# Choosing two of eight experts in two parts, in the stage ahead and behind the first products

## The reference

```python
logits = (xt @ w_gate.T).astype(jnp.float32)
top_logits, top_idx = jax.lax.top_k(logits, TOP_K)          # TOP_K = 2 of 8
top_gates = jax.nn.softmax(top_logits, axis=-1)
gates = (one_hot(top_idx, E) * top_gates[..., None]).sum(axis=1)
for e in range(E):
    h = xt @ w_in[e].T
    y = y + gates[:, e:e + 1] * (h @ w_out[e].T)
# x = x + 0.5 * y
```

## Time and profile before

| | us |
|---|---|
| median of three runs | 1414.59 |
| profiled execution, its own time | 1414.04 |
| its span | 1412.3 |
| PE busy | 1173.9 (83%) |
| DVE busy | 869.1 (62%) |
| ACT busy | 649.0 (46%) |
| POOL busy | 585.5 (41%) |

### The profile page before, as it was taken

The page is one execution under the profiler, slowest core; times in us unless marked ns, Lnnn a source line. Parts: engine busy times, 40 slices in busy tenths (PEclk is TensorE's granted clock), DMA queues, the critical chain, the costliest instruction groups (busy, mean ns, idle before and its releaser), DMA issues. The chain is left out here.

```text
span 1412.3 us, 30262 instructions
## 1 busy us (share of the span) xinstructions
PE 1173.9 (83%) x11551; PEld 686.9 (49%) x11561; DVE 869.1 (62%) x2263; ACT 649.0 (46%) x1346; POOL 585.5 (41%) x727
## 2 busy tenths in 40 slices
PE   3895889886968979999969886846985999898698
PEld 3582444444845645566536534333771233233377
DVE  5146778842155678788535598871177889893205
ACT  1222566651432446766632252421453777685143
POOL 5763244113541669987310112163743033123352
PEclk9997799997968989999989896867995799999699
DMA  7542333105710186666229000013433122110344
GB/s 138 154 113 79 94 105 98 45 11 141 223 41 1 38 231 193 181 190 200 78 39 112 8 2 1 3 46 109 132 95 101 47 80 80 34 37 17 87 143 119
DMA packets 137674, 128.66 MB, mean 91 GB/s; under 512 B 19245, under 2 KB 120377, under 8 KB 137536
## 3 DMA queue, kind: packets, MB, share of 16 engines
q1 hardware_dynamic: 127392, 103.46, 28.0%
q0 software_dynamic: 10080, 23.31, 5.0%
q10 hardware_dynamic: 64, 0.04, 0.0%
HBM read 79.80 MB, written 47.69 MB: 90 GB/s over the span
## 5 line engine op out<-in xcount | busy, mean ns | idle before, releaser
L2803 DVE TENSOR_REDUCE att_maxima<-psum 128x2 f32<-128x1024 f32 (+3 forms) x384 | 353.4, 950 | 78.2 <-PE psum L2496 32.7
L2695 ACT ACTIVATE att_probs<-psum 128x512 f32<-128x512 f32 (+1 forms) x640 | 323.6, 555 | 155.6 <-PE psum L2466 55.0
L124 POOL TENSOR_TENSOR rstd<-var_eps,neg_half 128x2 f32<-128x2 f32 x88 | 61.6, 704 | 335.9 <-DVE var_eps L97 332.4
L2449 PE MATMUL psum<-att_queries,att_keys 50*32 50x384 bf16 (+4 forms) x1280 | 159.2, 330 | 23.3 <-ACT att_probs L2695 11.3
L2455 PE MATMUL psum<-att_keys,att_queries 48*32 48x384 bf16 (+4 forms) x1280 | 157.5, 345 | 12.4 <-DVE att_maxima L2803 12.1
L1144 POOL DMA_INDIRECT returned<-moe_out,moe_slot_tokens x101 | 100.9, 999 | 108.7 <-DVE moe_out L1068 79.3
L926 ACT ACTIVATE moe_hidden<-psum,moe_b 128x320 f32<-128x320 f32 (+1 forms) x128 | 77.7, 607 | 112.2 <-PE psum L833 111.7
L2449 PEld LDWEIGHTS psum<-att_queries,att_keys 50*32 50x32 bf16 (+1 forms) x1280 | 46.2, 92 | 144.2 <-issue 69.8
L833 PE MATMUL psum<-moe_slot_columns,moe_w 128*128 128x320 f32 (+1 forms) x256 | 99.9, 535 | 3.1 <-ACT moe_slot_columns L921 2.9
L644 POOL DMA_INDIRECT dispatched<-normalised_rows,route_scatter_i x64 | 63.8, 998 | 80.7 <-DVE route_scatter_i L624 51.4
L840 PE MATMUL psum<-moe_w,moe_hidden 128*128 128x128 f32 x784 | 93.5, 277 | 0.0
(11 more groups left out here) (303 smaller groups left out, 2347.6 us busy)
## 6 DMA issues: line engine op xcount, KB each, us to landing
moe_w<-l_w SPq DMA_DIRECT2D x64, 256.0 KB, 3.1
score_terms<-att_parts SPq DMA_DIRECT2D x32, 384.0 KB, 2.7
moe_back<-returned SPq DMA_DIRECT2D x24, 256.0 KB, 4.2
att_queries<-score_terms SPq DMA_DIRECT2D x64, 96.0 KB
att_keys<-score_terms SPq DMA_DIRECT2D x64, 96.0 KB
att_queries<-score_terms SPq DMA_DIRECT2D x16, 384.0 KB, 4.2
att_keys<-score_terms SPq DMA_DIRECT2D x16, 384.0 KB, 5.5
score_terms<-att_parts POOLq DMA_DIRECT2D x12, 384.0 KB, 3.2
```

The lines of the kernel that those rows point to most:

```text
L2449: col = nc.tensor.matmul(g.psum[one, cols_bank + h, c0:c0 + w], k_op[own_rows, ci, p, key], q_op[own_rows, ci, p, first_query[s]:T], start ...
L2695: nc.scalar.activation(probs[:, G % 2, 2 * p + r, unit_at[u]:unit_at[u] + w], g.psum[:, cols_bank + r, 0:w], ACT.Exp).then_inc(probs_ready, 1)
L2803: ins = nc.vector.tensor_reduce(maxima[:, G % 2, t, 2 * p:2 * p + 2], g.psum[:, rows_bank(k):rows_bank(k) + 2, c0:c0 + w], axis=AX, op=ALU ...
```

## The change

A class `TopTwo` holds the choice; it makes it for a part of the tiles at a time: `choose(v, half, c)` finds the best (c = 0) or the second best (c = 1), `exponential(act, half)` and `weigh(v, half)` do the rest. `weight` and the semaphores live across stages; `weight` lies in the room of `expert_selector`.

For `ffn2_0` the parts are tiles 0 to 7 and 8 to 15. The first is chosen on DVE within `ffn1_1`, in its units (3,2), (3,3) and (3,4); the second in `ffn2_0` behind `add_pair(1, 0)`, and weighed behind `add_pair(1, 1)`. The last group of `ffn1_1` is only added and its mean and variance taken there; the root, its rows, its turning, columns and logits move into `ffn2_0`.

For `ffn2_1` the parts are tiles 0 to 11 and 12 to 15. The first is chosen and weighed at the end of `recurrence2`, behind the last `ln_rows`; the second in `ffn2_1` at the same places as in `ffn2_0`. At the end of `recurrence2` PE takes logits(2) ahead of turn(3), and ACT copy(2) ahead of columns(3).

```diff
 def ffn1(...)                                       # PE
-            ln_transpose(g, pe, ln, B - 1, xnt_bank, one_bank=True)
-            ln_logits(g, pe, ln, B - 1, xnt_bank)
+            if not top:
+                ln_transpose(g, pe, ln, B - 1, xnt_bank, one_bank=True)
+                ln_logits(g, pe, ln, B - 1, xnt_bank)
...                                                  # ACT, behind the last unit
+            if top:
+                top.exponential(act, 0)
             ln_copy_logits(g, act, ln, B - 2, xnt_bank)
...                                                  # DVE, in the units
+                if top and b == B - 1 and c in (2, 3):
+                    v.wait_ge(ln.logits, top.split)
+                    top.choose(v, 0, c - 2)
+                if top and (b, c) == (B - 1, chunks - 1):
+                    top.weigh(v, 0)
...                                                  # POOL
-            for b in range(B):
+            for b in range(B - 1 if top else B):
...
+class TopTwo:
+    def after(self, v, ins):
+        self.steps += 1
+        ins.then_inc(self.step, 1)
+        v.wait_ge(self.step, self.steps)
+
+    def choose(self, v, half, c):
+        g, at = self.g, self.tiles(half)
+        scores = g.logits if c == 0 else self.others
+        if c:
+            self.after(v, g.nc.vector.scalar_tensor_tensor(self.others[:, at, :], self.onehot[:, 0, at, :], MASKED,
+                                                           g.logits[:, at, :], ALU.mult, ALU.add))
+        for step in range(5):
+            self.after(v, first_max_step(g, step, scores[:, at, :], self.best[:, c, at], self.work[:, at, :],
+                                         self.onehot[:, c, at, :], self.tie[:, at]))
+        if c:
+            g.nc.vector.tensor_tensor(self.delta[:, at], ...).then_inc(self.exp_in, 1)
+
+    def exponential(self, act, half):
+        act.wait_ge(self.exp_in, half + 1)
+        self.g.nc.scalar.activation(self.delta[:, at], self.delta[:, at], ACT.Exp).then_inc(self.exp_out, 1)
+
+    def weigh(self, v, half):
+        v.wait_ge(self.exp_out, half + 1)
...                                                  # six instructions, the last to self.weight
 def ffn2(...)                                       # PE, in group 0 behind products 5 and 7
+                if closing and (b, at) == (0, 5):
+                    ln_transpose(g, pe, closing, B - 1, rank_bank)
+                if closing and (b, at) == (0, 7):
+                    ln_logits(g, pe, closing, B - 1, rank_bank)
...                                                  # ACT, group 0 and 1
+                if closing and b == 0:
+                    ln_columns(g, act, closing, B - 1, rank_bank)      # behind scale(0, 1)
...
+                if closing and b == 0:
+                    ln_copy_logits(g, act, closing, B - 1, rank_bank)  # behind scale(0, 3)
+                if b == 1:
+                    top.exponential(act, 1)                            # behind scale(1, 3)
...                                                  # DVE: the choice ahead of the first group goes
-            first_max(g, after, logits[:], best[:, 0, :], work[:], onehot[:, 0, :, :])
...
             for b in range(B):
+                if b == top.split:
+                    v.wait_ge(top.weighted, 2)
                 add_pair(b, 0)
+                if closing and b == 0:
+                    ln_rows(g, v, closing, B - 1)
+                if b == 1:
+                    if closing:
+                        v.wait_ge(closing.logits, B)
+                    for c in range(2):
+                        top.choose(v, 1, c)
                 if b >= 1:
                     add_shares(b - 1)
...
                 add_pair(b, 1)
+                if b == 1:
+                    top.weigh(v, 1)
...                                                  # POOL
+            if closing:
+                ln_rstd(g, pool, closing, B - 1)
...
 def recurrence2(...)
             turn(2)
+            logits(2)
             turn(3)
-            logits(2)
             logits(3)
...
             columns(2)
+            copy_logits(2)
             columns(3)
-            copy_logits(2)
             copy_logits(3)
+            top.exponential(act, 0)
...
             ln_rows(g, v, ln, 3)
+            v.wait_ge(ln.logits, top.split)
+            for c in range(2):
+                top.choose(v, 0, c)
+            top.weigh(v, 0)
...
 def program(...)
+        top = TopTwo(g, "top2_0", 2)
+        top_again = TopTwo(g, "top2_1", 3)
```

More of the change, by code:

```diff
@@ L1389, in _ @@
                 begin_more()
-            ln_columns(g, act, ln, B - 1, xnt_bank)
-            ln_copy_logits(g, act, ln, B - 1, xnt_bank)
+            if not top:
+                ln_columns(g, act, ln, B - 1, xnt_bank)
+                ln_copy_logits(g, act, ln, B - 1, xnt_bank)
             if begun:
@@ L1462, in _ @@
                 begun.rest_from_bank(v, 2, 0, cb_bank)
-            ln_rows(g, v, ln, B - 1)
+            if not top:
+                ln_rows(g, v, ln, B - 1)
             if begun:
@@ L1488, in _ @@
                 begun.low(pool, 1, 1)
+        return ln
 class ExpertProducts:
@@ L1521, in copy, with __init__, room, tiles @@
             self.g.nc.scalar.copy(self.products[:, i, :], banks[i][:]).then_inc(self.copied, 1)
-def ffn2(g, name, products, gate=None, prefetch=None, routing=None, begun=None):
+class TopTwo:
+    def __init__(self, g, name, split):
+        sem = semaphores(g, name)
+        self.g, self.split = g, split
+        self.step, self.weighted = sem("step"), sem("weights")
+        self.exp_in, self.exp_out = sem("exp_in"), sem("exp_out")
+        room = g.expert_selector[:].rearrange("p c t -> p (c t)").bitcast(F32)
+        self.weight = room[:, 0:TILES * E].rearrange("p (t e) -> p t e", e=E)
+        self.steps = 0
+    def room(self, sb):
+        self.others, self.work = sb("others_top", [P, TILES, E]), sb("work_top", [P, TILES, E])
+        self.best, self.tie = sb("best_top", [P, 2, TILES]), sb("tie_top", [P, TILES])
+        self.onehot = sb("onehot_top", [P, 2, TILES, E])
+        self.delta, self.denom = sb("delta_top", [P, TILES]), sb("denom_top", [P, TILES])
+        self.gates = sb("gates_top", [P, 2, TILES])
+    def tiles(self, half):
+        return (slice(0, GROUP * self.split), slice(GROUP * self.split, TILES))[half]
+    def after(self, v, ins):
[12 more added lines that the diff above has]
+        if c:
+            g.nc.vector.tensor_tensor(self.delta[:, at], self.best[:, 1, at], self.best[:, 0, at], ALU.subtract
+                                      ).then_inc(self.exp_in, 1)
+    def exponential(self, act, half):
+        at = self.tiles(half)
+        act.wait_ge(self.exp_in, half + 1)
+        self.g.nc.scalar.activation(self.delta[:, at], self.delta[:, at], ACT.Exp).then_inc(self.exp_out, 1)
+    def weigh(self, v, half):
+        ops, at = self.g.nc.vector, self.tiles(half)
+        wide = [P, at.stop - at.start, E]
+        spread = lambda c: self.gates[:, c, at, None].to_broadcast(wide)
+        v.wait_ge(self.exp_out, half + 1)
+        self.after(v, ops.tensor_scalar(self.denom[:, at], self.delta[:, at], 1.0, None, ALU.add))
+        self.after(v, ops.reciprocal(self.gates[:, 0, at], self.denom[:, at]))
+        self.after(v, ops.tensor_tensor(self.gates[:, 1, at], self.delta[:, at], self.gates[:, 0, at], ALU.mult))
+        self.after(v, ops.scalar_tensor_tensor(self.work[:, at, :], self.onehot[:, 0, at, :], 0.5, spread(0), ALU.mult, ALU.mult))
+        self.after(v, ops.scalar_tensor_tensor(self.others[:, at, :], self.onehot[:, 1, at, :], 0.5, spread(1),
+                                               ALU.mult, ALU.mult))
+        ops.tensor_tensor(self.weight[:, at, :], self.work[:, at, :], self.others[:, at, :], ALU.add).then_inc(self.weighted, 1)
@@ L1525, in ffn2 @@
+def ffn2(g, name, products, top, gate=None, prefetch=None, routing=None, begun=None, closing=None):
     nc, a = g.nc, g.a
@@ L1644, in _ @@
         def _(v):
[L1645 to L1650, removed]
-            first_max(g, after, logits[:], best[:, 0, :], work[:], onehot[:, 0, :, :])
[L1653 to L1664, removed]
+            v.wait_ge(top.weighted, 1)
             def add_pair(b, turn):
@@ L1815, in add_bias, with recurrence2 @@
                                        ).then_inc(self.biased, 1)
-def recurrence2(g, name, begun, gate):
+def recurrence2(g, name, begun, gate, top):
     nc, weights = g.nc, begun.weights
@@ L3120, in program @@
             begun = RecurrenceStart(g, ctx, "rec2", weights)
-            ffn2(g, "ffn2_0", products, prefetch=weights, begun=begun)
-            recurrence2(g, "rec2_ends", begun, gate[2])
+            ffn2(g, "ffn2_0", products, top, prefetch=weights, begun=begun, closing=closing)
+            recurrence2(g, "rec2_ends", begun, gate[2], top_again)
         routes = held.enter_context(ExitStack())
@@ L3125, in program @@
```

(2 more changed lines are left out.)

31 lines of the change are left out of this document (14 added, 17 removed).

## The result

The changed kernel takes 1419.95 us (median of 20 runs, 1413.41 to 1431.84), the kernel before 1410.96 (20 runs, 1403.04 to 1416.67): ratio 1.0063, 95% interval 1.0047 to 1.0079. It is 9.0 us slower by the medians; the forecast was 8.7. The forecast time was 1422.7, in a range of 1416.0 to 1426.5. The measured one lies 2.8 lower, because the kernel before took 1410.96 in this comparison and not the 1414.04 on which the forecast was added up. The two profiled executions differ by less (spans 1412.3 and 1415.8), as the stages that were not touched took 1.4 us less ahead and 4.9 less behind in the one of after. In the twelve profiled executions of this document these unchanged stages behind took 455.9 to 463.5 us, with a mean granted PE clock of 0.90 where they were short and 0.89 where they were long.

The account below looks back on a forecast made before the run. DVE was taken as the bound from `add_pair(1, 0)` on, with the choice covering PE's slow first products. Terms -3.6 + 5.0 + 3.9 + 3.4 = +8.7 us on 1414.04 gave 1422.7 us, range 1416.0 to 1426.5.

Parts of the forecast that it names:

- End of `ffn1_1`: End of `ffn1_1`: insertions delay the last add by 1.3 us, yet the next stage starts 3.6 us earlier.
- `ffn2_0`: First changed stage: slow first products uncovered and second choice on DVE's path; group 2 at 25.7 us for 20.8, loses 5.0.
- Recurrence: End of `recurrence2`: choice, changed order and Exp's table load start the next stage at 888.2 for 884.34; loses 3.9 us.
- `ffn2_1`: Second changed stage: as in `ffn2_0` without the moved work; group 2 at 24.0 us behind its start for 20.6, loses 3.4.
- T + 4: Head of `ffn2_0`, starting at T: PE's clock starts at half and rises 4 us later; `ffn2_1` taken the same.
- 0.86: PE's products in `ffn2_0`: 12 take 10.57 us at full clock, read as 0.86 us each, 1.72 at half.
- Warm products: Rival: PE's clock is up, or rises at once, at both heads; 2 x 2.0 us less, 1418.7 us; chance 0.15.
- Slack: Rival: second parts behind the first products come free, as DVE isn't what group 1 waits for; 1414.5 us; chance 0.12.
- The drain: Rival: a drain of about 1380 ns follows the table load ahead of Exp at `recurrence2`'s end; 1424.1 us; chance 0.05.

Follow-up runs that it names:

- head_choice: Kernel before with only `ffn1_1` and `ffn2_0` changed, tiles 0 to 7 chosen at the head of `ffn2_0`, last logits behind the tenth product; ratio to before 0.9979.
- table_early: Changed kernel plus a one-column Exp on ACT ahead of the recurrence's first columns; touched stretch 165.39 us (changed kernel 170.30).
- choice_repeated: Changed kernel with the first maximum of the second part found four times, 15 more DVE steps per stage; touched stretch 176.84 us (changed kernel 170.30).
- clock_kept: Changed kernel plus unread bf16 products on PE, 11 behind `ffn1_1` and 7 behind the recurrence's last logits; ratio to before 1.0045.
- turned_as_before: Only `ffn1_1` and `ffn2_0` changed against the kernel before, but the last group still normalised, turned and gated in `ffn1_1`; touched stretch 165.51 us (before 160.55).

## Why the prediction was right

The way, the mechanism and nearly the size held. Its terms, in its order, each from one execution:

- *End of `ffn1_1`*: forecast -3.6, measured -3.94. The steps of eight tiles took 0.26 as interpolated (five from 793.72 to 795.00), PE's wait for the hidden chunk 0.47, and the cost of the insertions is 1.1 by head_choice (1.3 forecast).
- *`ffn2_0`*: +5.0, measured +5.62. The first adds came at 2.2 and 3.8 us (2.1 and 3.8 forecast), the tenth product's reader at 13.0 (12.15).
- *Recurrence*: +3.9, measured +3.81. The load stood where it was put and cost 1.4.
- *`ffn2_1`*: +3.4, measured +4.13; the reader at 11.9 (10.9).

The two terms that were short share one mis-sized step: "I let it rise at T + 4". It rose at 5.5 and 6.0 us. Every us at half clock delays products by half a us, so 0.75 and 1.0. The tenth product's reader came 0.8 and 1.0 late; what followed took some 0.2 less than forecast in each stage, so 0.6 and 0.7 were left. The sum is 9.75 for 8.7; 0.15 lies behind group 2 of `ffn2_1`. That the number came so near is in part luck: with the same two stages in table_early the clock rose at 2.9 and 3.6, and group 2 came 2.6 us sooner in the two together. T + 4 lies in the middle of what was seen.

One reading is loose: 10.57 us for 12 products are 0.88 each. The 0.86 that the sums use is the distance between two starts, which is what their steps need.

Warm products: the mechanism is real, its price 2.8 us in `ffn2_0` (2.0 forecast, against a rise at 4 and not at 5.5), but PE had to be kept busy for it; without that both heads began at half clock in every trace, and at the second head it didn't help. Slack: refuted by choice_repeated. The drain: Exp began 1.29 us behind the load's start in after; in before another function began 1.30 behind the earlier trace rows. So the Trainium skill's further 1380 ns (ScalarE: Activation LUTs, What ACT_TABLE_LOAD costs) doesn't show here.

The loss, then, in measured parts: the choice covered the slow first products at both heads, and taken from there it uncovered them; its second parts came back whole on the engine that bounds the stage (4.2 and 3.7 us, from the first step to the last in after); and at the second seam it held up a stage that PE had entered at once. Against that stands the move behind the first products, worth 3.1. The first and last of these causes are shown by runs that undo them (head_choice, clock_kept, turned_as_before) and the second parts by choice_repeated. At the second seam the load is shown by table_early; that the choice there cost the rest of the 3.8 is read from the rows.

## What to carry to other kernels

Before a serial piece (a chain in which each instruction waits for the one before) is taken from the head of a stage, ask what else runs beside it: here PE needed those microseconds to fill its banks at half clock, and the piece was nearly free. Idle time ahead of a point where all engines wait for each other is free only while the work in it ends before the last engine does. Splitting a chain of small instructions pays its fixed part twice (0.26 us a step for eight tiles, 0.32 for sixteen), so the second part must fall into a real gap.

## What was not expected of the hardware

The clock's rise behind a start is not a constant of the code: with the same instructions group 2 of `ffn2_0` came 25.06 or 26.41 us behind the start (rise at 2.9 and 5.6), that of `ffn2_1` 23.57 to 24.78 (3.6 and 6.0). In clock_kept 11 bf16 products held a clock that was high over a pause, but seven more behind a stage at half clock did not raise it: PE worked from 880 to 889.6 with 0.69 us of pause before it rose.
